# Token stages of a two-layer decoder as straight code, with products and turns moved to other heads and banks

## The reference

```
x = layernorm(x + linear(x))          # L0: weights with masked 32x32 blocks, bias
x = layernorm(x + cross_attention(x, ctx, mask))
x = layernorm(x + gated_slot_ffn(x))  # L0: top 8 of 256 slots, softmax, two projections, gelu gate
x = layernorm(x + self_attention(x))  # L1: attends over the batches, causal
x = layernorm(x + cross_attention(x, ctx, mask))
x = layernorm(x + routed_ffn(x))      # L1: top 16 of 64 experts of rank 8
```

## Time and profile before

| | us |
|---|---|
| median of 3 runs | 3921.38 (3917.74 to 3926.45) |
| profiled execution | 3914.28 |
| its span on the core | 3912.5 |
| PE busy (matmuls) | 3326.9, 85% of the span |
| DVE busy | 1840.5, 47% |
| ACT busy | 1327.8, 34% |
| POOL busy | 835.4, 21% |

### The profile page before, as it was taken

The page is one execution under the profiler, slowest core; times in us unless marked ns, Lnnn a source line. Parts: engine busy times, 40 slices in busy tenths (PEclk is TensorE's granted clock), DMA queues, the critical chain, the costliest instruction groups (busy, mean ns, idle before and its releaser), DMA issues. The chain is left out here.

```text
span 3912.5 us, 67365 instructions
## 1 busy us (share of the span) xinstructions
PE 3326.9 (85%) x25342; PEld 2675.9 (68%) x25342; DVE 1840.5 (47%) x4774; ACT 1327.8 (34%) x3539; POOL 835.4 (21%) x700
## 2 busy tenths in 40 slices
PE   3888888888479999999947999999996388888887
PEld 2666676676268887788825888888884277676775
DVE  4566666667432222333224233332223477676775
ACT  1566566666110111111101111111010466666663
POOL 1122122211042223233202323333321000000000
PEclk9999999999589999999966999999998699999998
DMA  5655455543221111111122111111111654454441
GB/s 189 165 154 156 129 152 147 153 129 95 50 71 45 41 43 43 48 54 54 32 54 65 49 43 54 54 54 54 43 38 29 163 134 125 115 128 113 125 120 39
DMA packets 190014, 346.78 MB, mean 89 GB/s; under 512 B 27873, under 2 KB 145217, under 8 KB 189778
## 3 DMA queue, kind: packets, MB, share of 16 engines
q1 hardware_dynamic: 186032, 341.00, 32.5%
q10 hardware_dynamic: 3746, 2.79, 0.2%
HBM read 272.19 MB, written 71.51 MB: 88 GB/s over the span
## 5 line engine op out<-in xcount | busy, mean ns | idle before, releaser
L733 ACT ACTIVATE L_probs<-L_masked,L_least 112x375 f32<-112x375 f32 x1024 | 624.4, 610 | 504.8 <-DVE L_least L813 500.8
L813 DVE CUSTOM_DVE_ANT_0 L_masked<-L_scores,L_nmask 112x375 f32<-112x375 f32 x1024 | 552.3, 543 | 344.4 <-PE L_scores L541 320.8
L546 PE MATMUL L_turned<-L_ident,L_probs 112*125 112x112 f32 x3072 | 568.4, 296 | 96.5 <-ACT L_probsT L729 46.0
L546 PEld LDWEIGHTS L_turned<-L_ident,L_probs 112*125 112x125 f32 x3072 | 472.1, 200 | 206.8 <-issue 76.4
L1359 PE MATMUL sa_feat<-sa_x_hi,heads_w_hi 128*128 128x512 f32 (+1 forms) x1536 | 570.2, 371 | 28.2 <-POOL heads_w_lo L1332 28.2
L1359 PE MATMUL sa_feat<-sa_x_hi,heads_w_lo 128*128 128x512 f32 (+1 forms) x1536 | 568.0, 370 | 0.0
L1359 PE MATMUL sa_feat<-sa_x_lo,heads_w_hi 128*128 128x512 f32 (+1 forms) x1536 | 564.6, 368 | 0.0
L541 PE MATMUL L_scores<-L_krep,L_qrep 128*112 128x376 f32 x1024 | 435.4, 426 | 16.5 <-ACT L_probs L733 8.5
L1464 DVE TENSOR_TENSOR sa_acc<-sa_acc,sa_ring 128x512 f32<-128x512 f32 x224 | 154.2, 689 | 463.1 <-PE sa_ring L1387 463.1
L1387 PE MATMUL sa_ring<-heads_p_hi,heads_o_hi 128*128 128x512 f32 x896 | 354.3, 395 | 0.0
L1387 PE MATMUL sa_ring<-heads_p_hi,heads_o_lo 128*128 128x512 f32 x896 | 353.2, 394 | 0.0
(11 more groups left out here) (293 smaller groups left out, 5471.5 us busy)
## 6 DMA issues: line engine op xcount, KB each, us to landing
L_qrep<-query_parts SPq DMA_DIRECT2D x256, 224.0 KB, 5.7
heads_raw<-in_wqkvU_dram SPq DMA_DIRECT2D x96, 512.0 KB, 3.5
L_krep<-ctx_parts SPq DMA_DIRECT2D x256, 188.0 KB, 3.8
heads_raw<-in_wprojU_dram SPq DMA_DIRECT2D x64, 512.0 KB, 3.5
query_parts<-L_qT_hi SPq DMA_DIRECT2D x64, 224.0 KB, 2.8
query_parts<-L_qT_lo SPq DMA_DIRECT2D x64, 224.0 KB, 3.6
L_xcur<-x SPq DMA_DIRECT2D x32, 448.0 KB, 3.6
L_val<-in_ctx_dram SPq DMA_DIRECT2D x64, 187.5 KB
```

The costliest lines, as they stand in the source:

```text
L546: mm = pe.transpose(turned[0:TC, m % 2, S * j:S * j + S], probs[0:S, m % 4, TC * j:TC * j + TC], ident[0:S, 0:S])
L733: nc.scalar.activation(probs[0:S, n % 4, :], masked[0:S, n % 3, :], ACT.Exp, bias=least[0:S, n:n + 1], scale=-1.0, accum_out=rsum[0:S, n:n ...
L813: v.tensor_tensor_reduce(out=masked[0:S, n % 3, :], in0=scores[0:S, n % 3, 0:T], in1=nmask[0:S, :], scale=1.0, scalar=HUGE, op0=ALU.add, o ...
```

## The change

- `turns`: no loop any more; all 20 bodies of each stage are straight code, and the semaphores count through. `take_off` is no longer called there.
- Query turns, both layers: the first half at step 28 with lag 2, the second at step 1 with lag 1 (before: steps 1 and 4 with lag 1 in layer 0, 27 and 30 with lag 2 in layer 1). ACT's and DVE's parts and SP's store of the first half move with them; in layer 0 that store now ends a body.
- Linear part: 6 products a step from steps 11 and 17 (before: 5 a step from 10 and 16); DVE's additions at 16 and 22, statistics at 17 and 23, normalization at 26.
- Layer 0 slot part: query product at 25, gate products at 26 to 28 into `spare` (before: 23, 26 to 29, `wide[0]`); gate read at 30, then the query copy, and the route product at step 0 of the next body; the top 8 and what follows it at steps 4 to 10; slot turn at 11; slot product at step 16 into the tail of a `turned` bank (before: step 8, `spare`).
- Layer 1: a second `row` buffer; `zg` at 30, its turn at step 0; output products at 4 to 7 into `spare` and at 11 to 13 into `wide[1]` (before: 2 to 5 and 6 to 9, `wide[0]` and `spare`); `res` at 8 and 14, its statistics at 10 and 16, normalization at 20; `row` turned at 16 and 17; `r` products at 21, `a` products at 23 to 28.

```diff
-        row = sb("row", [P, D])
+        row = sb("row", [P, 1 if first else 2, D])
...
         def turns(eng, body):
             w = Counts(eng)
-            for t in range(-2, 2):
+            for t in range(-2, B + 2):
                 body(t, w, live(t))
-            w.take_off()
-            with eng.Fori(0, (B - 4) // TURNS) as i:
-                w = Counts(eng)
-                for j in range(TURNS):
-                    body(TURNS * i + j + 2, w, live(2))
-                w.take_off()
...
+            return w
+
+        Z_HEAD, ROWS = 12, 1 if first else 2
...
-        if first:
-            Q_TURN, Q_HI, Q_LO, Q_DONE = ((1, 1), (4, 1)), ((2, 1), (5, 1)), ((3, 1), (7, 1)), (9, 1)
-        else:
-            Q_TURN, Q_HI, Q_LO, Q_DONE = ((27, 2), (30, 2)), ((28, 2), (31, 2)), ((29, 2), (0, 1)), (2, 1)
+        Q_TURN, Q_HI, Q_LO, Q_DONE = ((28, 2), (1, 1)), ((29, 2), (2, 1)), ((30, 2), (3, 1)), (9, 1)
...
+                if on(1):
+                    store_queries(w, t + 1, 1)
                 if first and on(1):
-                    store_queries(w, t + 1, 0)
...
-                if not first and on(2):
+                if on(2):
                     store_queries(w, t + 2, 0)
...
-                for h, n0 in ((0, 10), (1, 16)):
-                    if n0 <= n < n0 + 5 and on(2):
-                        i = 5 * (n - n0)
+                for h, n0 in ((0, 11), (1, 17)):
+                    if n0 <= n < n0 + 4 and on(2):
+                        i = 6 * (n - n0)
...
                 if on(-2):
                     if n == 0:
-                        pe.wait_ge(gate_h_read, w.next(gate_h_read))
-                    if n == 5:
+                        pe.wait_ge(qaug_ok, w.next(qaug_ok))
+                        pe.matmul(spare[0:S, :], qaug[:, :], route[:, :], start=True, stop=True).then_inc(route_ok, 1)
+                    if n == 11:
                         pe.wait_ge(slot_w_ok, w.next(slot_w_ok))
...
-                    if n == 23:
+                    if n == 25:
                         pe.wait_ge(lo2_ok, w.next(lo2_ok))
-                        products(spare[0:BOT, 0:S], (wq_hi, wq_lo), (tT_hi, tT_lo), slice(0, S), KT, 0, 3 * KT).then_inc(query_ok, 1)
-                    if n == 27:
-                        pe.wait_ge(qaug_ok, w.next(qaug_ok))
-                        pe.matmul(spare[0:S, :], qaug[:, :], route[:, :], start=True, stop=True).then_inc(route_ok, 1)
-                    if 26 <= n < 30:
-                        i = 6 * (n - 26)
-                        mm = products(wide[0:S, 0, 0:UH], (tT_hi, tT_lo), (wu_hi, wu_lo), slice(0, UH), KT, i, i + 6)
+                        products(spare[0:BOT, UH:UH + S], (wq_hi, wq_lo), (tT_hi, tT_lo), slice(0, S), KT, 0, 3 * KT)
+                    if 26 <= n < 29:
+                        i = 8 * (n - 26)
+                        mm = products(spare[0:S, 0:UH], (tT_hi, tT_lo), (wu_hi, wu_lo), slice(0, UH), KT, i, i + 8)
...
+            def slot_values(w):
+                pe.wait_ge(wT_ok, w.next(wT_ok))
+                for j in range(2):
+                    mm = pe.matmul(turned[0:S, Z_HEAD % 2, TJ * S:TJ * S + BOT], wT[:, j, :], u_val[:, j, :],
...
+                    if 4 <= n < 8:
+                        i = 3 * (n - 4)
+                        mm = products(spare[0:S, :], (z_hi, z_lo), (b_hi, b_lo), slice(0, 512), 4, i, i + 3)
+                    if 11 <= n < 14:
+                        i = 4 * (n - 11)
+                        mm = products(wide[0:S, 1, :], (z_hi, z_lo), (b_hi, b_lo), slice(512, 1024), 4, i, i + 4)
...
+                    if n in (16, 17):
+                        pe.wait_ge(out_read, w.next(out_read))
                 if on(-1):
-                    if n == 15:
+                    if n == 16:
                         pe.wait_ge(x2_ok, w.next(x2_ok))
-                        tokens_turned(w, 0, spare)
+                        tokens_turned(t, 0, spare)
...
-                if on(-1) and n == 25:
-                    act.wait_ge(query_ok, w.next(query_ok))
-                    nc.scalar.copy(qaug[0:BOT, :], spare[0:BOT, 0:S]).then_inc(qaug_ok, 1)
-                if on(-1) and n == 29:
+                if on(-1) and n == 30:
+                    act.wait_ge(gate_h_read, w.next(gate_h_read))
+                    nc.scalar.copy(qaug[0:BOT, :], spare[0:BOT, UH:UH + S]).then_inc(qaug_ok, 1)
+                if on(-2) and n == 3:
                     act.wait_ge(route_ok, w.next(route_ok))
...
-                if on(-2) and n in (7, 11):
+                if on(-2) and n in (8, 14):
...
-                if n in (15, 21):
-                    h = n // 21
+                if n in (16, 22):
+                    h = n // 22
```

206 lines of the change are left out of this document (95 added, 111 removed).

## The result

The changed kernel takes 3928.5 us (median of 20 runs, 3922.5 to 3939.9) against 3920.9 for the kernel before (20 runs on the same chip). The ratio is 1.0024, 95% interval 1.0017 to 1.0031: slower by 0.24%. One of the 20 executions of the kernel before took 4130.8 us, in a slower state of the chip, and is not in the ratio. The forecast was 3760 us, with 3690 to 3860 as its range and 0.05 for slower.

A forecast was written before the change was run, and what follows sets the result against it. It took the PE to bound most of the kernel, DVE and ACT layer 0's first 11 heads; 33 + 55 + 80 - 7 = 161 us off 3921 gave 3760 us, range 3690 to 3860.

The forecast's parts named there:

- Loops, 33 us: Turns 2 to 13 of both stages leave the loop, without its crossing waits: 33 us saved, ends 29 and 37.
- rival (c): Straight code starves the engines through instruction fetch; slower, 4000 us at 2.5 us a packet; chance 0.05.
- Layer 0, from head 11 on, 0.7 us: Layer 0's last 21 heads: token-split and attention-read waits go, a linear wait grows; 0.7 us a turn saved.
- Layer 0, heads 0 to 10, 3.0 us: Layer 0's first 11 heads, bound by DVE and ACT: 18.94 to 15.9 us, 3.0 us a turn saved.
- (a): Only the loops count, since removed waits come back at the next semaphore; 60 us saved, 3860 us; chance 0.19.
- Layer 1, 5.0 us a turn: Layer 1: shorter PE waits, less half-clock and light-step loss; 5.0 us a turn saved, 80 us in 16 turns.
- Start and tail, -7: Later load of transposed tokens in the first two turns costs 5 us, layer 0's tail 2 us; -7 together.
- Rival (b): PE clock stays up in both layers' half-clock stretches; 69 us more saved, 3690 us; chance 0.12.

The follow-up runs named there:

- N1: Changed kernel with most of GpSimd's x_lo and of the residual's second half left out in layer 0, result incomplete: 3896.2 us, ratio 0.9942.
- X3: Changed kernel with one added 512-column product before each four router products of layer 1, six a turn: 3947.8 us, ratio 1.0065.
- X2: Changed kernel with layer 1's 24 router products spread over three steps, two wide bottleneck products ahead in each: 3901.3 us, ratio 0.9956.

## Why the prediction was wrong

*Loops, 33 us.* Right in kind, and too small: 39 us, just above the bounds 29 to 37. No "issue" wait is left, and rival (c) is out: instruction fetch moved no more packets than before (121 and 81 of its two kinds in the whole span, against 129 and 107), and no straight turn waits for it.

*Layer 0, from head 11 on, 0.7 us.* Failed, by a small sum: that part of an ordinary turn went from 35.7 to 36.0 us. The listed waits went as listed: token split and attention read gone, a new wait of the linear products of up to 1.0 us, forecast as 0.9. Not listed was the wait for ACT's `L_oT`, 13.7 us in 16 turns.

*Layer 0, heads 0 to 10, 3.0 us.* **This step failed**, in the line that gave DVE "about 14.9 us of work". It counted instructions at their durations in the old order. I put pen and slot_w where they lie in the new one and did not look at what GpSimd does there: x_lo and the residual each hold one of them up, 1.8 and 0.8 us a turn. These heads took 18.6 us, for 15.9 forecast. With the collision out they take 16.0 and the turn 51.4 (N1), against 50.9 forecast: the steps were sound, a resource was missing. The trace of before could have shown it: `L_left`, on the same 112x256 elements as pen, took 882 ns where pen took 426. (a) is answered in part. Without the collision the PE still waits 61.2 us for ACT's copies, 29.0 before, so waits did move there as (a) has it; but they did not eat the gain, N1's stage is 28.7 us below that of the loops alone. Of 15 turns at 3.7 us that is half: the second and the fifteenth turn grew (50.3 to 51.2, 43.3 to 45.7), and in two the clock was down.

*Layer 1, 5.0 us a turn.* **Failed twice.** Of the size: a turn of the new order at full clock takes 45.1 to 45.7 us where 43.1 was forecast, so the order is worth 2.4 to 3.0 us a turn and not 5.0. The waits went from 5.1 to 3.2, forecast 2.4; and the PE's busy time of a turn at full clock fell by 0.6 us (43.09 to 42.48), where half clock and light steps had been booked at 1.7 and 0.8. Over the stage it is 26 us (746.7 with the loops alone, 720.4 with the outputs spread) to 36 (710.6), not 80: the first two turns grew. And in its sign: I booked "what the PE lost at half clock after the 2.0 us wait, up to 1.7 us" as a gain, as if a shorter wait could only help the clock. In the old order (an ordinary turn of the run with the loops alone, from 3443.6) the PE stood still for 1.7 us at step 15, the clock was at half for 3.4 us behind it, and it was back at full 1.6 us ahead of the router products. Now the light stretch lies at steps 14 to 20, right in front of them. The clock falls 0.9 us after step 21 has begun and stays at 1.2 GHz for 10.2 us, through nearly all of the 24 and some 3 us beyond them, though the PE is busy throughout. Steps 21 to 23 take 10.6 us there and 6.1 in the lucky turn; the 10.2 us of PE work at half clock are about 5 at full (an estimate, by halving). The 5 us lost are more than the waits that the change had taken out of the turn (5.1 to 3.2).

*Start and tail, -7.* The start came 6.0 us later, forecast 5; the number is right in part by luck. Straight code alone moved it by 2.4 (the run with the loops alone), which the sum had nowhere. With x split earlier the other 3.6 were gone, and moving the store back as well changed nothing. Whether it was the earlier x_hi or x_lo ahead of the bias addition wasn't separated, and the store was not moved back by itself. The tail of layer 0, forecast 2 us longer, was not: from its last score product to layer 1's first one it took 2126.1 us, 2129.2 before.

*Small slips in the working.* DVE and ACT are 64 to 70% busy in the two stages, not 58 to 70. Half of 2.7 us in 16 turns is 22 us, not the 25 given as layer 1's lower end, and the 105 at its upper end is not worked out. Neither moves the forecast.

The gap closes. The terms gave stages of 861.7 - 16 - 55 = 791 and 763.3 - 17 - 80 = 666 us; they stand against 844 and 787: 53 + 121 = 174 us, against 3928.5 - 3760 = 168.5. Of it 31 at most are the collision (844 - 813, N1), about 67 the clock in layer 1 (787 - 720, the run with the outputs spread alone). The rest, 22 in layer 0 and 54 in layer 1, is the order's own worth taken too large.

Rival (b) had the right cause in the wrong direction: it let the clock only stay up. A rival in which a rearranged turn puts a light stretch in front of narrow products, and the clock stays down through them, belonged on the slower side. Rival (c), which held that side, was the weakest that the trace offered.

What stays open: what makes the clock fall. The lucky turn has the same steps and the same light stretch as the others (the PE stands still for 0.9 us at step 19 in both), and its clock did not fall; so the light stretch alone does not make it fall, though with work spread into the stretch the fall went out of most turns. Open too: why the router products hold the clock down when wide ones added among them (X3) do not raise it, while X2 did gain; and why the filler in layer 1 left the fall in some turns.

## What to carry to other kernels

When an instruction moves, ask what the other engines do at its new place, not only how long it took at the old one: for DVE instructions on SBUF, look at GpSimd's row of the timeline first. And when waits go out of a kernel that the PE bounds, look at how the PE's work is spread over the turn as well as at its sum. Removing 2 us of waits a turn was worth less than where the light stretch came to lie; spreading twelve products over five steps instead of three gave 66 us. Compare turns of one kernel with each other: the one turn of 45.7 us among those of 50.4 and 51.8 told what the order is worth without the fall of the clock. And compare instructions of one size: here the one that took twice as long as its like had a neighbour on GpSimd.
